# Block 1's normalisation root on ScalarE too, with eps as the bias of the square root, in a fused attention and feed-forward block

## The reference

```
xn  = (x - mean) / sqrt(var + 1e-5)                      # per token
h   = tanh(xn @ W1.T + b1);  s = h @ w2 + b2             # a score per token
e   = exp(s - max over the sequence)
ctx = cumsum(e * xn) / cumsum(e)                         # along the sequence
attn = tanh(concat(ctx, xn) @ Wc.T + bc)
g = xn @ (w_gate/127).T;  u = xn @ (w_up/127).T          # 256 -> 768, int32 weights
ffn = (silu(g) * u) @ (w_down/127).T                     # 768 -> 256
out = x + attn + ffn
```

## Time and profile before

| | |
|---|---|
| median of three runs | 393.72 us |
| profiled execution: its time, its span | 393.06 us, 391.1 us |
| TensorE busy | 385.9 us (99%) |
| VectorE, ScalarE, GpSimd busy | 297.5 (76%), 235.6 (60%), 210.1 (54%) |
| 768 matmuls of 512 columns (`Gg`, `Gu`) | 177.3 us as shown, 379 ns each with their modelled end |
| granted TensorE clock, mean | 1.0 of full speed |

### The profile page before, as it was taken

One profiled execution on the slowest core, in us unless ns is written; L12 is line 12 of the kernel. 1 busy time (PEld: TensorE's weight loads), 2 busy tenths in 40 slices (PEclk: granted clock), 3 DMA queues, 4 the chain that ended last, 5 costly groups with the idle time before them and its releaser, 6 DMA issues.

```text
span 391.1 us, 7885 instructions
## 1 busy us (share of the span) xinstructions
PE 385.9 (99%) x2740; PEld 268.7 (69%) x2740; DVE 297.5 (76%) x632; ACT 235.6 (60%) x434; POOL 210.1 (54%) x289
## 2 busy tenths in 40 slices
PE   8999999999999999999999999999999999999996
PEld 4556676757566686866877676767677676676765
DVE  6799998999996997876769966777676765754351
ACT  4766576689985659786556575364553644536250
POOL 1487586874629989794335405866456554502000
PEclk9999999999999999999999999999999999999999
DMA  8944525576834232475210005043231220100001
GB/s 275 348 158 69 137 53 134 106 189 89 201 72 96 54 83 81 116 165 97 76 34 29 27 28 164 28 128 87 58 72 55 90 85 26 54 28 28 28 28 61
DMA packets 54945, 36.56 MB, mean 93 GB/s; under 512 B 31858, under 2 KB 50292, under 8 KB 54900
## 3 DMA queue, kind: packets, MB, share of 16 engines
q1 hardware_dynamic: 54608, 35.73, 35.5%
q10 hardware_dynamic: 292, 0.26, 0.2%
HBM read 20.19 MB, written 8.45 MB: 73 GB/s over the span
## 4 chain that ended last, share of the span: by engine, by line
PE 97%; DVE 2%; issue 0%; DVEq 0%
PE bank L707 44%; PE bank L743 41%; PE bank L763 9%; PE bank L1381 1%; DVE ex L1121 0%; DVE stats L951 0%; PE bank L700 0%; PE bank L1377 0%; DVE veps L980 0%; DVE xt L1091 0%; DVE bank L1116 0%; DVE sg L1413 0%; PE bank L813 0%; DVE mv L955 0%; PE bank L819 0%
## 5 line engine op out<-in xcount | busy, mean ns | idle before, releaser
L743 PE MATMUL bank<-xt,narrow 128*128 128x512 f16 x768 | 177.3, 379 | 0.0
L743 PEld LDWEIGHTS bank<-xt,narrow 128*128 128x128 f16 x768 | 75.2, 98 | 75.4 <-DVE wide L1121 0.2
L707 PE MATMUL bank<-narrow,wide 128*128 128x256 f16 x792 | 96.4, 273 | 0.0
L707 PE MATMUL bank<-narrow,xt 128*128 128x256 f16 x768 | 92.8, 273 | 0.3 <-DVE xt L1091 0.3
L707 PEld LDWEIGHTS bank<-narrow,xt 128*128 128x128 f16 x768 | 75.0, 98 | 19.0 <-DVE xt L1091 0.6
L1258 POOL TENSOR_TENSOR wide<-ex,wide 128x512 f16<-128x512 f32 x32 | 39.4, 1248 | 87.6 <-ACT wide L909 87.6
L888 ACT ACTIVATE sg<-bank 128x512 f32<-128x512 f32 x96 | 57.2, 596 | 46.3 <-PE bank L743 45.6
L1116 DVE SCALAR_TENSOR_TENSOR bank<-bank,sg 128x512 f32<-128x512 f32 x96 | 66.1, 694 | 24.4 <-PE bank L743 21.3
L707 PEld LDWEIGHTS bank<-narrow,wide 128*128 128x128 f16 x792 | 77.5, 98 | 9.4
L895 ACT ACTIVATE wide<-bank 128x512 f16<-128x512 f32 x90 | 53.3, 596 | 47.7 <-DVE bank L1116 39.3
L1121 DVE TENSOR_TENSOR wide<-bank,wide 128x512 f16<-128x512 f32 x90 | 60.5, 678 | 9.9 <-ACT wide L895 8.6
(11 more groups left out here) (103 smaller groups left out, 262.3 us busy)
## 6 DMA issues: line engine op xcount, KB each, us to landing
rows<-scratch SPq DMA_DIRECT2D x16, 512.0 KB, 5.1
out_y<-xres SPq DMA_DIRECT2D x31, 256.0 KB, 2.1
xres<-in_x SPq DMA_DIRECT2D x15, 512.0 KB, 5.1
xt<-xt SPq DMA_TRANSPOSE x56, 2.5
wide<-in_wg SPq DMA_DIRECT2D x1, 768.0 KB, 5.9
wide<-in_wu SPq DMA_DIRECT2D x1, 768.0 KB, 8.4
wide<-in_wd SPq DMA_DIRECT2D x1, 768.0 KB, 10.1
wide<-in_wc SPq DMA_DIRECT2D x1, 512.0 KB, 11.1
```

What stands on the lines that cost most here:

```text
L707: return pe.matmul(dst, lhs, rhs, start=False, stop=stop, skip_group_check=True)
L743: mm = pe.matmul(b[:, :], pg.up(which, k, j), pg.xn(sx, k, tok), start=n == 0, stop=n == len(todo) - 1)
```

## The change

1. The square root on ScalarE reads the variance and adds eps as its bias (a new tile `eps`, one memset). `veps` falls away in this form, and `minus_half` is one instruction. Block 1 gets this form too (`ROOTS = 2`): step `Rq` 1 on ScalarE, `root_first(dve, 1)` on VectorE, no `T` 1 on GpSimd.
2. `Tb` stands behind `Rq` 1, since a table for the root is to be loaded once. So `Th` and `Sg` of block 0 stand behind it too.
3. The bias rows have a bank each (7 and 6). The scores' `Ss` of block 0 reads `b1` out of the bank, and `Ea` and `Eb` copy the rows later.
4. 9 warm-up matmuls for 12; the two fill matmuls behind `Lb` are gone.
5. The plan's table follows, and the order of all engines is computed anew.

```diff
+ROOTS = 2
-    "Ea": (SE, 0.5, 0.63), "Tb": (SE, 1.4, 1.5), ...
+    "Ea": (SE, 0.3, 0.43), "Eb": (SE, 0.3, 0.43), "Tb": (SE, 1.4, 1.5), "Rq": (SE, 0.2, 0.3), ...
...
+ROW_BANKS = (BANKS - 1, BANKS - 2)
-BEGIN = {TE: 7.3, SE: 5.7, VE: 8.1, PO: 1.0, SY: 12.0}
+BEGIN = {TE: 7.0, SE: 5.95, VE: 7.9, PO: 1.0, SY: 12.0}
-X_SENT = (0.0, 11.1, 20.0)
+X_SENT = (0.0, 10.3, 20.0)
...
     if kind == "Tb":
-        return [(("Xh", 0, 1), 0)]
+        return [(("Xh", 0, 1), 0), *((("Rq", g, 0), 0) for g in range(1, ROOTS))]
+    if kind == "Rq":
+        return [(("B", i, 1), 0)]
...
-        return [(("B", blocks[-1], 1), 0), *([(("R", i - 1, 0), 0)] if i > 1 else [])]
+        return [(("Rq", i, 0) if i < ROOTS else ("B", blocks[-1], 1), 0), *([(("R", i - 1, 0), 0)] if i > 1 else [])]
...
     if kind == "Th":
-        return [(("S", i, x), 0)]
+        return [(("S", i, x), 0), *([] if i or wide else [(("Tb", 0, 0), 0)])]
...
-        WARM, FILL = 12, 2
+        WARM, FILL = 9, 2
...
+        def square_root(act, g):
+            act.wait_ge(v_mv, 2 * g + 2)
+            act.activation(rstd[:, columns(g)], mv[:, columns(g), 1], ACT.Sqrt, bias=eps[:, 0:1]).then_inc(a_root, 1)
...
             elif kind == "Ss":
-                act.wait_ge(a_b, 1)
                 act.wait_ge(p_warm, 1)
-                bias_seed(act, pg, 0, open_bank(act, pg, "S", i, n), a_ss)
+                if i or pg.wide:
+                    act.wait_ge(a_b, 1)
+                    bias_seed(act, pg, 0, open_bank(act, pg, "S", i, n), a_ss)
+                else:
+                    act.wait_ge(p_b, 1)
+                    spread_row(act, pg, bank[ROW_BANKS[0]][:, 0:D], open_bank(act, pg, "S", i, n), a_ss)
...
             elif kind == "Ea":
                 act.wait_ge(p_b, 1)
-                act.activation(every[:, 0:2 * D], bank[BANKS - 1][:, :], ACT.Copy).then_inc(a_b, 1)
+                act.activation(b1_every, bank[ROW_BANKS[0]][:, 0:D], ACT.Copy).then_inc(a_b, 1)
+            elif kind == "Eb":
+                act.wait_ge(p_b, 2)
+                act.activation(w2b, bank[ROW_BANKS[1]][:, 0:D], ACT.Copy).then_inc(a_b, 1)
+            elif kind == "Rq":
+                square_root(act, i)
...
-            dve.wait_ge(v_mv, 2)
-            step(dve.tensor_scalar(veps[:, t], mv[:, t, 1], EPS, None, ALU.add))
-            dve.tensor_scalar(minus_half[:, t], veps[:, t], -0.5, None, ALU.mult)
-            dve.wait_ge(a_root, 1)
+            dve.wait_ge(v_mv, 2 * g + 2)
+            dve.tensor_scalar(minus_half[:, t], mv[:, t, 1], EPS, -0.5, ALU.add, ALU.mult)
+            dve.wait_ge(a_root, g + 1)
...
-                root_seed(dve, i)
+                root_seed(dve, i) if i >= ROOTS else root_first(dve, i)
...
+                    if i < ROOTS:
+                        ins = pool.tensor_scalar(normed(pg, i, k)[:, t, :], xres[:, c, :], mv[:, c, 0:1], rstd[:, c:c + 1],
+                                                 ALU.subtract, ALU.mult)
...
-            act.wait_ge(v_rs0, 1)
-            act.activation(rstd[:, columns(0)], veps[:, columns(0)], ACT.Sqrt).then_inc(a_root, 1)
+            square_root(act, 0)
...
             pe.wait_ge(s_b, 16)
+            to_every(bank[ROW_BANKS[0]], b_row)
             pe.wait_ge(s_w2, 16)
-            to_every(bank[BANKS - 1], 0, b_row)
-            to_every(bank[BANKS - 1], D, w2_row).then_inc(p_b, 1)
+            to_every(bank[ROW_BANKS[1]], w2_row)
...
-                if (kind, i, n) == ("Lb", 0, 1):
-                    for n in range(FILL):
-                        warm_up(spare_bank)
...
+            dve.memset(eps[:, :], EPS)
-            root_first(dve)
+            root_first(dve, 0)
```

More of the change, by code:

```diff
@@ L187, in due_times @@
             due["R", g, 0] = root
-            for n in range(NEWTON):
+            if g < ROOTS:
+                due["Rq", g, 0] = root
+            for n in range(NEWTON * (g >= ROOTS)):
                 due["T", g, n] = root + 0.1 + 1.4 * n
@@ L217, in due_times @@
             due["Ch", i, k], due["Cl", i, k] = ctx - 10.0 + 2.4 * k, ctx - 9.3 + 2.4 * k
[L218 removed]
+    for st, t in {"W1h": -4, "Ea": due["Th", 0, 0] - 0.5, "Eb": due["Sv", 0, 0] - 0.5, "Tb": end["S", 0, 0] - 0.4, "W1l": -3, "K1": 40, "Wgh": -4, "Wuh": -2, "Wdh": 3, "Kg": 215, "Kh": 217, "Ku": 219, "Kx": 221, "Kd": 220, "Ke": 222, "Ky": 224,
                   "Kc": 42, "Kf": 230, "Kp": 233, "Fl": 233, "Wch": 60, "Wcl": 61, "BrT": 999, "BrS": 999, "BrV": 999,
@@ L275, in needs @@
             frees = [(("Xm", i - 2, x), 0)]
-        return [(("T", g, NEWTON - 1), 0), *frees, *([(("C", 1, 1), 0)] if i == SPARE_TO - 1 and not wide else [])]
+        return [(("T", g, NEWTON - 1) if g >= ROOTS else ("R", g, 0), 0), *frees, *([(("C", 1, 1), 0)] if i == SPARE_TO - 1 and not wide else [])]
     if kind == "Lb":
@@ L294, in needs @@
     if kind == "Th":
-        return [(("S", i, x), 0)]
+        return [(("S", i, x), 0), *([] if i or wide else [(("Tb", 0, 0), 0)])]
+    if kind == "Sv" and i == 0 and not wide:
+        return [(("Th", i, x), 0), (("Eb", 0, 0), 0)]
     if kind == "Sv":
@@ L298, in needs @@
     if kind == "Ss" and i == 0 and not wide:
-        return [(("Ea", 0, 0), 0), *([(("Xh", 0, 0), 0)] if x else [])]
+        return [(("Xh", 0, 0), 0)] if x else []
+    if kind == "Ss" and i == 1 and not wide:
+        return [(("Ea", 0, 0), 0)]
     if kind in ("Gg", "Gu"):
@@ L362, in __init__ @@
         self.place, self.before, self.held = {}, {}, dict.fromkeys(range(BANKS))
-        self.whole = {n: not wide and n < BANKS - 1 for n in range(BANKS)}
-        self.open_now, self.freed = set(), {n: 9.0 if n == BANKS - 1 else 0.0 for n in range(BANKS)}
+        self.whole = {n: not wide and n not in ROW_BANKS for n in range(BANKS)}
+        self.open_now, self.freed = set(), {n: 11.0 if n in ROW_BANKS else 0.0 for n in range(BANKS)}
         self.behind, self.freed_behind = set(), set()
@@ L1387, in _ @@
             pe.wait_ge(s_b, 16)
+            to_every(bank[ROW_BANKS[0]], b_row)
             pe.wait_ge(s_w2, 16)
-            to_every(bank[BANKS - 1], 0, b_row)
-            to_every(bank[BANKS - 1], D, w2_row).then_inc(p_b, 1)
-            spare_bank = next(FITS.place["Gg", 0, j] for j in range(KH) if FITS.before["Gg", 0, j] is None and FITS.place["Gg", 0, j] < BANKS - 1)
+            to_every(bank[ROW_BANKS[1]], w2_row)
+            spare_bank = FITS.place["Lb", 0, 0]
             for n in range(FILL):
```

72 lines of the change are left out of this document (40 added, 32 removed).

## The result

The changed kernel is slower: 395.84 us (median of 5 runs, 395.38 to 396.20) against 393.72 us (5 runs, 392.94 to 394.10), a ratio of 1.006 with a 95% interval of 1.0049 to 1.0071. The forecast was 392.9 us with a range up to 393.9. The profiled execution took 395.64 us (span 393.8 us; before 393.06 and 391.1).

A forecast was written before the change was run, and what follows sets the result against it. TensorE, busy 99% of the span, bounds the kernel. Terms -0.36 - 0.49 + 0.18 = -0.67 us give 393.05 from the 393.72 median; with 0.15 allowed for fewer warm-ups, 392.9 us, own range 392.5 to 393.4, overall 392.0 to 393.9.

The forecast's parts named there:

- The step that failed: Block 1's root: GpSimd has the first half normalised by 15.6 us, TensorE reaches it at 17.42; cost none.
- rival 3: Start: nine warm-ups and idle time delay TensorE's clock rise or let it fall; 395.0 us, chance 0.04.
- Term 1: Start: an earlier root chain and earlier `Xh` bring the first score to 8.76 us from 9.12; -0.36 us.
- The table: ScalarE's table load moves behind block 1's root, to 12.31 us from 10.02; TensorE's wait costs nothing.
- Term 2: TensorE's hole at 24.54 us, a wait for block 1's `Xl` on VectorE, goes away; -0.49 us.
- Term 3: First `D`: a new wait for `Hl` 5, behind block 3's seeds held by GpSimd; +0.18 us.
- I take nothing: Behind 33 us: matmuls and nearly all of the order stay the same, so nothing is counted; bound 0.3 us.

The follow-up runs named there:

- experiment 3: Two kernels: the changed kernel with block 1 normalised by multiply-add, then by add-multiply, instead of subtract-multiply; 395.04 and 395.28 us.
- the first kernel of 8: The changed kernel with block 1 by add-multiply, block 3's root due 2 us later, twelve warm-ups, two fill matmuls behind the first transposes, none ahead; 393.06 us.
- Experiment 1: The kernel before with only block 1's four GpSimd normalisations turned into subtract-multiply; 395.69 us, ratio 1.0055.
- experiment 9: The changed kernel with twelve warm-ups instead of nine, block 1 still normalised by subtract-multiply; 396.24 us, ratio 1.0066.
- experiment 8: Two twelve-warm-up versions of the changed kernel: add-multiply with block 3's root later, and block 1's root by seed and Newton steps; 393.06 and 393.04 us.

## Why the prediction was wrong

**The step that failed** is the one on block 1's root: "In either case GpSimd has the first half of block 1 normalised (2.19 us for both) by 15.6 [...] Cost: none." I took 2.19 us from the row of multiply-add for four instructions that the diff turns into subtract-multiply, and gave no bound for it. The same row in the changed kernel has 4.85 us, from 14.96 to 19.81, and costs TensorE 1.94 us at the second half and 0.22 at the first. With the old duration it would have ended at 17.15, and `Lb` 1, due at 17.3, would have waited for nothing, as in the profiles of experiment 3 and of the first kernel of 8. Experiment 1 shows that this edit alone makes 2.4 us. No rival of mine had this mechanism; rival 3 came nearest to the measured time (395.0 for 395.84), by another cause.

**Term 1** (-0.36) held in its kind, and came out larger by luck. The first score came at 8.66 for 9.12. Of these 0.46 us, 0.20 are luck: VectorE's first statistics start at 3.37 for 3.57, because x landed earlier in this execution. The rest, 0.26, stands against 0.36 forecast: the root starts 0.21 earlier against the statistics, as said, but takes 0.30 us for 0.20, with eps as a column. The Trainium skill, "ScalarE: Activation LUTs", "What ACT_TABLE_LOAD costs", gives about 93 ns for each such column; the trace agrees with 0.10.

**The table** came at 13.10 for 12.31 forecast, since x of block 1 landed 7.6 us after its issue and not 6.9. `Th` followed at 14.50, and no TensorE step waited for it. The next ACTIVATE stands right behind the load, at 14.39, as it did before the change.

**Term 2** held: the hole of 0.49 at 24.54 is gone, block 2's `veps` took 0.17 us (22.36), and no wait for `Xl` came in its place.

**Term 3** was mis-sized: 0.71 us for 0.18. The order was right: `veps` of block 3 took 0.99 us, up to the end of GpSimd's `Xm` (31.40 + 2.27 = 33.67), and `Hl` 5 followed at 34.22. But `Xm` did not move with block 2's root, whose seeds end 0.74 us earlier than before (23.01 for 23.75) while `Xm` starts 1.34 later. It waits 2.04 us for ScalarE's `Xh` (the last row of GpSimd above), and by this sum it kept its distance to TensorE's work: 33.67 less the first score and less the 1.94 us lost ahead of it is 23.07, for 31.35 - 8.76 = 22.59 forecast. These 0.48 us are nearly all of the error of 0.53.

**"I take nothing"** for what comes behind 33 us was wrong too, by 0.91 us and so by more than my bound of 0.3. At 101 to 103 us two of the four seeds of an 8-column root were held for 1.01 us each:

```profile
101.15 1.01 DVE L1014 TENSOR_SCALAR minus_half<-veps 128x8 f32<-128x8 f32 x1
...
102.27 1.01 DVE L1016 TENSOR_SCALAR rstd<-seed 128x8 int32<-128x8 int32 x1
```

Before, one was held there, and the reduction of the score maxima stood ahead of the seeds, at 100.31. Now it stands behind them and came at 103.92; it frees the bank that TensorE opens next, at 104.26, where 0.56 us were lost. The other 0.35 us, at 108.89, are a wait for ScalarE's `Sg`, whose cause stays open. The order there had changed; "nearly all of the order is the same" was true and not enough.

**Rival 3**, the late clock at 0.04, was judged too rare. The rise beyond the first transposes is real with nine warm-ups: 8 of 12 runs of the kernel before, so changed, are above 394, and the profile of one of them has it. I argued from one profile in which the clock rose at 5.39. The prediction's citation that the number of slow matmuls differs from run to run (the Trainium skill, "TensorE: Matmul & The Clock Gate", Part 1) is now borne out by rows: behind the same first nine matmuls, in one execution each of nine-warm-up kernels, the rise stands at 4.35, 4.82, 5.35 and 5.60 us, and at 10.20 to 10.96. In the changed kernel itself a late clock would have cost little, by experiment 9, and its profile has none.

**What is left of the forecast.** With the failed step mended, block 3's root moved and twelve warm-ups (experiment 8), the first score comes at 8.85 and the median is 0.3 us under the kernel before, within the noise. The forecast of -0.67 us (terms 1 to 3) isn't shown by any kernel here.

Not settled: why one of eleven runs of each kernel of experiment 8 is still 1.1 to 1.5 us above the next one, when the clock rises late, and whether the mended kernels are faster than before by the 0.3 us that their medians show.

## What to carry to other kernels

Price an instruction by a row with the same pair of operations, not only the same engine, shape and type; where no such row exists, take the next slower one as the upper bound and see what waits for it. After mending one wait, look for what it had covered: here a late clock, worth up to 1.5 us at the first score, can hide behind 1.9 us of waiting. And judge warm-up by many executions, since one profile shows only one rise of the clock, and ask in the same way when the loads landed: x of block 1 landed between 6.3 and 8.1 us after its issue in the profiles of these kernels.

## What was unexpected of the hardware

On GpSimd, tensor_scalar on 128x256 f32 has two speeds by its pair of operations: 0.56 us for multiply-add, add-multiply and multiply-multiply, 1.23 us for subtract-multiply, multiply-subtract and add-add. In this shape, subtracting a column costs 0.67 us more than adding its negative, which one VectorE instruction of 0.16 us for four columns prepares. Small VectorE operations on 128x4 and 128x8 that take 0.17 us otherwise lasted up to 1.06 us while GpSimd worked, a tensor_tensor among them (from 13.33 us to the end of GpSimd's `Wuh` at 14.38), and 1.41 us in the profile of experiment 9. Not every one is held: the reciprocal at 13.12 us took 0.18 beside the same `Wuh`.
